# A perceiver block on one core: column term as a single fp32r product, first batch's norm earlier, correction's rows during the attention

## The chip, the cores and the metric

One NeuronCore of a Trainium2 chip runs the whole program as one launch. The metric is the device time of a launch in microseconds (us), median over the runs. TensorE (PE) multiplies, VectorE (DVE) and ScalarE (ACT) do elementwise work and move results out of PSUM, GpSimd (POOL) fills masks, and SyncE (SP) issues nearly all transfers from memory. Each engine works through its own list in order and waits on semaphores.

## The reference, cut to what matters

Two batches of 128 rows by 2048 columns go through three residual steps.

```python
x = x + fake_quant(layernorm(x)) @ fake_quant(ctx)         # ctx: 2 x 2048 x 2048, 33.5 MB of fp32
h = layernorm(x); q = h @ Wq; k, v = split(h @ Wkv)         # 32 heads of 64, one shared k and v
x = x + softmax(q k^T/8 + alibi, causal) v @ Wo
x = x + layernorm(x) @ (scales * (nibbles(qweight) - (nibbles(qzeros) + 1))) + bias
```

`fake_quant` rounds to the integers 0 to 255 and subtracts a zero point z. The kernel works on values shifted by 128, so the true product is that of the shifted integers plus a row term plus a **column term**: (128 - z1) times the column sums of the shifted context. The last step's zero points and bias are added by a small product with the groups' row sums, the **correction**.

## The kernel before, in words

All work is written out by hand as one list per engine.

**First step, contexts.** SP loads 32 context tiles of 128x2048 fp32 (1 MB each) into a ring of eight slots, 16 for each batch. For each, ACT quantises to bytes (`round_ctx`, L411), DVE converts the bytes to bf16 into one of two buffers (`convert_ctx`, L679), and PE runs four 512-column products into the batch's banks (L956) and four 32-row products with ones that gather the column sums in one bank (L963). `convert_ctx(i)` waits for PE to have finished tile i-2; PE's tile i waits for `convert_ctx(i)`.

After a batch's last tile, `colsums(b)` (L685) copies the column sums out, and `zero_point(b)` (L970) multiplies them by a selector `sel` that holds 128 - z1 in one row for each chunk, four fp32 products, adding the column term to the batch's four banks. DVE then adds each chunk to the residual and takes its statistics (`first_residual`, L690 and L597), and normalises (L611).

**Hand over.** `transposes(n)` (L988) turns a normalised batch: 16 transposes in four groups, each group into a bank. ACT copies a group out as its upper fp32r part (`upper`, L424), DVE subtracts for the lower part (`remainder`, L618, which counts `lo_out`). Groups 0 and 3 share a bank for both batches, so the last four transposes wait for the remainder of group 0. For batch 0 they stand between context tiles of batch 1 (before `ctx_tile(1, 8)`); ACT's `upper(0, g)` stand after `round_ctx(25)` and `round_ctx(26)`. For batch 1 they stand between q products.

**Second step.** Weights come as 1 MB granules; ACT makes the upper part (`upper_w`, L433), DVE the lower (`remainder_w`, L627). The first four q granules are multiplied piece by piece: `q_by_upper(w, b)` (L1008, eight products), `q_by_lower(w, b)` (L1015, four). `keys_values` (L1041 to L1048) then forms k and v of both batches. From there a chain runs: DVE copies them out (L760, L761), ACT issues two transfers that double k (L521), waits for them, fills `k_pair` (L526), and only then copies batch 1's q rows out of PSUM (`q_rows(1)`, L443), for which PE's second half of granule 4 waits.

**Output weights and correction.** After the attention POOL zeroes the tiles of the correction (L395, L396, in `work`, where the probabilities were), SP loads zero points and scales (L320, L321) behind the eleventh output granule, DVE unpacks and multiplies them (L884 to L888), SP adds the bias rows (L327), ACT rounds (L565) and DVE splits (L898). PE uses the result at L1171. SP's list is in order, so each of its waits holds what stands behind it.

The last step runs 16 granules of dequantised weights (L1138), made by DVE and ACT, against both batches.

Lines the argument touches in the lists:

```python
for w in range(3):          # PE, L1195
    q_by_upper(w, 0)
transposes(1)
...
q_by_upper(3, 1)            # PE, L1206
keys_values()
q_by_lower(3, 0)
q_by_lower(3, 1)
value_rows()
```

Of the kernel before, what the change touches and what calls it, by code (L numbers as in the profile page):

```python
# [16 lines left out]
B = 2  # L17
# [49 lines left out]
def perceiver(nc, x, ctx_in, s1, z1, s2, z2, wq, wkv, wo, qweight, qzeros, scales, bias, out):  # L67
# [6 lines left out]
    with ExitStack() as ec:  # L74
# [9 lines left out]
        with nc.sbuf_tensor("nib_pad", [P, D], F32), nc.sbuf_tensor("nib_a", [P, D], F32) as nib_a, \  # L84
                nc.sbuf_tensor("raw_fifth", [P, D], F32) as raw_fifth, \
                nc.sbuf_tensor("corr_r", [P, D], F32R) as corr_r:
            pass

# [26 lines left out]
        with nc.sbuf_tensor("sel", [P, NCH, P], F32) as sel:  # L115
            pass
# [31 lines left out]
        part_lo = sb("part_lo", [P, 2], F32)  # L148
        one_row = sb("one_row", [P, 1], F32)
# [4 lines left out]
        colsum_at = work[:, 0, 2 * CH:3 * CH]  # L154
        prob_slots = [work[:, 1, 0:D // 2], work[:, 1, D // 2:D], work[:, 0, D // 2:D]]
        corr = work[:, 0]
        corr_z = work[:, 1]
# [45 lines left out]
        sel_zero = sem("sel_zero")  # L203
# [59 lines left out]
        def tr_bank(n, g):  # L263
            if n == 0:
                return g % 3
            return 1 + g % 3 if n == 1 else 4 * (n % B) + g
# [16 lines left out]
        @block.sync  # L283
        def _(sp):
            sp.dma_start(resid[:, 0, :], x[0]).then_inc(x_loaded[0], 16)
            for i in range(CTX_TILES):
                if i == 6:
                    sp.dma_start(resid[:, 1, :], x[1]).then_inc(x_loaded[1], 16)
                if i >= CTX_RING:
                    sp.wait_ge(ctx_q, i - CTX_RING + 1)  # L290
                sp.dma_start(ctx_slots[i % CTX_RING], ctx_tiles[i]).then_inc(ctx_loaded[i % CTX_RING], 16)

            def load_granule(rows, base, w):
                slot_free(sp, w)
                n, kq = divmod(w - base, 4)
                sp.dma_start(raw_slots[slot_of(w)].rearrange("p (t n) -> p t n", t=4),
                             rows[:, 4 * kq:4 * kq + 4, n * CH:(n + 1) * CH]).then_inc(w_loaded[slot_of(w)], 16)

            for w in range(W_Q, W_O):
                if w < RING:  # L300
                    sp.wait_ge(ctx_q, CTX_TILES - CTX_RING + w + 1)
                if w == RING:
                    sp.wait_ge(a16_set, 2)
                    sp.dma_start(kv_raw[:].rearrange("p (t n) -> p t n", t=KT), wkv_rows).then_inc(wkv_loaded, 16)
                load_granule(wq_rows, W_Q, w)
                if w in (9, 13):
                    h = (w - 9) // 4
                    for i in range(GROUPS // HALVES):
                        g = h * (GROUPS // HALVES) + i
                        sp.dma_start(scale[i * PER_GROUP:(i + 1) * PER_GROUP, h, :],  # L310
                                     scales[g:g + 1, :].to_broadcast([PER_GROUP, D])).then_inc(scales_loaded[h], 16)
            for w in range(W_O, W_O + 11):
                load_granule(wo_rows, W_O, w)


            attention_over(sp)
            sp.wait_ge(corr_zero, 1)
            for blk in range(3):
                r = slice(CBLK * blk, CBLK * blk + GROUPS)
                sp.dma_start(zraw[r, :], qzeros).then_inc(corr_loaded, 16)  # L320
                sp.dma_start(corr[r, :], scales).then_inc(corr_loaded, 16)  # L321
            for w in range(W_O + 11, W_O + 14):
                load_granule(wo_rows, W_O, w)
            sp.dma_start(packed[:, 0, :], qweight[0:P, :]).then_inc(packed_loaded[0], 16)
            sp.wait_ge(corr_set, 1)
            for blk in range(2):
                sp.dma_start(corr[CBLK * blk + GROUPS:CBLK * blk + GROUPS + 1, :],  # L327
                             bias.unsqueeze(0)).then_inc(bias_loaded, 16)
            load_granule(wo_rows, W_O, W_O + 14)
            load_granule(wo_rows, W_O, W_O + 15)  # L330
            sp.dma_start(packed[:, 1, :], qweight[P:2 * P, :]).then_inc(packed_loaded[1], 16)

            for b in range(B):
                for n in range(NCH):
                    c = slice(n * CH, (n + 1) * CH)
                    sp.wait_ge(final_set, NCH * b + n + 1)
                    sp.dma_start(out[b, :, c], resid[:, b, c]).then_inc(stored, 16)
            sp.wait_ge(stored, 16 * B * NCH)

        @block.gpsimd  # L340
        def _(pool):
            steps = [0]

            def link(ins):
# [12 lines left out]
                                    pattern=[[-1, P]], channel_multiplier=1).then_inc(idents_set, 1)  # L357

# [35 lines left out]
            attention_over(pool)  # L394
# [4 lines left out]
        def _(act):  # L399
# [162 lines left out]
            for w in range(W_O + 6, W_O + 14):  # L562
                upper_w(w)
            act.wait_ge(bias_loaded, 16 * 2)
            nc.scalar.activation(corr_r[:], corr, ACT.Copy).then_inc(corr_hi, 1)  # L565
            upper_w(W_O + 14)
            upper_w(W_O + 15)
# [15 lines left out]
        def _(dve):  # L583
# [53 lines left out]
            def selector():  # L637
                dve.wait_ge(prm_set, 1)
                nc.vector.memset(sel[:], 0.0).then_inc(sel_zero, 1)
                dve.wait_ge(sel_zero, 1)  # L640
                for n in range(NCH):
                    r = slice(P // NCH * n, P // NCH * n + 1)
                    ins = nc.vector.tensor_scalar(sel[r, n, :], sel[r, n, :], dif[r, 1:2], None, ALU.add)
                ins.then_inc(sel_set, 1)
# [36 lines left out]
            def colsums(b):  # L681
# [3 lines left out]
                nc.vector.tensor_copy(colsum_at, bank[:, COLSUM_BANK[b], :]).then_inc(colsum_out, 1)  # L685
# [41 lines left out]
            convert_ctx(KT + 3)  # L727
            convert_ctx(KT + 4)
            reciprocal_sd(2)
            normalise(0).then_inc(norm_set, 1)  # L730
            for i in range(5, 8):
                convert_ctx(KT + i)
            for g in range(4):
                remainder(0, g)
                if g < 3:
                    convert_ctx(KT + 8 + g)
            for i in range(11, 14):
                convert_ctx(KT + i)
# [137 lines left out]
            for i in range(7, 11):  # L876
                remainder_w(W_O + i)
# [8 lines left out]
            link(ins)  # L886
            link(nc.vector.tensor_scalar(corr_z[rows, :], zi, -1.0, 7.0, ALU.mult, ALU.add))
            nc.vector.tensor_tensor(corr[rows, :], corr[rows, :], corr_z[rows, :], ALU.mult).then_inc(corr_set, 1)  # L888
            second_residual(1, 0)
# [8 lines left out]
            nc.vector.scalar_tensor_tensor(out=corr_r[:], in0=corr_r[:].bitcast(F32), scalar=part_lo[:, 0:1],  # L898
# [42 lines left out]
        def _(pe):  # L941
# [25 lines left out]
            def zero_point(b):  # L967
                pe.wait_ge(colsum_out, b + 1)
                for n in range(NCH):
                    mm(bank[:, 4 * b + n, :], sel[:, n, :], colsum_at, start=False,  # L970
                       stop=True).then_inc(ctx_done, 1)

            def transposes(n):
                b = n % B
                pe.wait_ge(norm_set, n + 1)
                for t in range(KT):
# [7 lines left out]
                    if n < B and t == 12:  # L984
                        pe.wait_ge(lo_out, 4 * n + 1)
# [201 lines left out]
            for k in range(KT):  # L1187
                if k == KT // 2:
                    transposes(0)
                ctx_tile(1, k)  # L1190
            zero_point(1)

            for w in range(3):  # L1195
# [10 lines left out]
            q_by_upper(3, 1)  # L1206
            keys_values()
            q_by_lower(3, 0)
# [101 lines left out]
```

## Time and profile before

| what | value |
|---|---|
| median of 3 runs (lowest, highest) | 424.68 us (423.73, 426.18) |
| profiled execution: its own time, its span | 425.28 us, 423.4 us |
| PE busy, weight loads busy | 374.8 us (89%), 275.9 us |
| DVE, ACT, POOL busy | 318.5 us, 223.6 us, 9.2 us |
| HBM read, over the span | 74.91 MB, 182 GB/s |
| chain that ended last: PE, DVE, ACT, DMA | 74%, 16%, 4%, 2% |

The span is the profiled execution from its first to its last record; the 1.9 us beside it belong to the launch. Times inside the span are counted from its start. PE's busy time is what the profile models for pipelined matmuls, so it is read together with the idle time ahead of a group, which names what ended the wait. PEclk is the clock granted to TensorE as a share of 2.4 GHz. A record of DVE that doesn't wait starts some 0.08 us before the end of the one ahead, and one that does starts 0.03 to 0.05 us behind what it waits for.

### The profile page before, as it was taken

To read this page: it belongs to the slowest core of one execution; us is meant where nothing else is said; L and a number is where in the kernel's file an instruction comes from. 1 tells how busy PE (TensorE), PEld (TensorE's weight loads), DVE (VectorE), ACT (ScalarE), POOL (GpSimd) and SP (SyncE) were. 2 spreads that over 40 slices of the span, in tenths; PEclk is the share of its full clock that TensorE was granted. 3 is DMA by queue.
4 is the path that set the end of the run, shared out by engine and by line. 5 is a ranking of instruction groups with operands and counts; after the bars stand their busy time and mean duration, and the time that the engine had idled before them with its cause. 6 is when DMAs were issued, how large, how long until landed. Compare 5 with 4: busy or idle time off the path is not lost.

```text
span 423.4 us, 4567 instructions
## 1 busy us (share of the span) xinstructions
PE 374.8 (89%) x1772; PEld 275.9 (65%) x1772; DVE 318.5 (75%) x354; ACT 223.6 (53%) x268; POOL 9.2 (2%) x43
## 2 busy tenths in 40 slices
PE   0167595878898999999999999999999999999996
PEld 0112131325786877877877867888888788888884
DVE  2598989768963394594595786679999899999922
ACT  1898888795334495297377465336605234444000
POOL 6000000000000000000000002000000000000000
PEclk9998999999999999999999999999999999999999
DMA  8999999995083294393436520987400000000033
GB/s 325 426 423 421 418 421 423 420 392 201 4 293 113 99 231 167 123 249 125 167 132 206 190 100 2 318 231 294 195 0 2 0 2 0 0 2 0 2 99 99
DMA packets 24273, 77.43 MB, mean 183 GB/s; under 512 B 1626, under 2 KB 1802, under 8 KB 19210
## 3 DMA queue, kind: packets, MB, share of 16 engines
q1 hardware_dynamic: 24084, 77.01, 50.4%
q8 instruction: 14, 0.23, 0.2%
q10 hardware_dynamic: 168, 0.13, 0.1%
q14 instruction: 7, 0.06, 0.0%
HBM read 74.91 MB, written 2.10 MB: 182 GB/s over the span
## 4 chain that ended last, share of the span: by engine, by line
PE 74%; DVE 16%; ACT 4%; issue 3%; DMA 2%; ACTq 0%; DVEq 0%
PE bank L1138 20%; PE bank L995 12%; PE bank L997 11%; PE bank L996 11%; DVE q L679 5%; PE bank L956 4%; PE bank L1076 3%; DVE stats L597 2%; PE bank L1008 2%; PE bank L1100 2%; ACT q L411 2%; PE bank L1015 2%; PE bank L1088 1%; DMA prm_row<-in_L_xattn_x_zp 1%; DVE resid L690 1%
## 5 line engine op out<-in xcount | busy, mean ns | idle before, releaser
L627 DVE TENSOR_TENSOR w_lo<-raw,w_hi 128x2048 fp32r<-128x2048 f32 x29 | 65.9, 2285 | 12.2 <-ACT w_hi L433 12.2
L433 ACT ACTIVATE w_hi<-raw 128x2048 fp32r<-128x2048 f32 x29 | 55.2, 1912 | 27.8 <-DMA raw<-in_L_attn_Wo 15.6
L1138 PE MATMUL bank<-w_hi,hd 128*128 128x512 f32 x208 | 52.6, 390 | 0.0
L956 PE MATMUL bank<-q,at 128*128 128x512 bf16 x128 | 36.8, 414 | 16.6 <-DVE q L679 16.3
L1138 PEld LDWEIGHTS bank<-w_hi,hd 128*128 128x128 f32 x208 | 39.0, 188 | 8.1
L679 DVE TENSOR_SCALAR q<-q 128x2048 bf16<-128x2048 uint8 x32 | 38.4, 1218 | 6.4 <-PE bank L963 3.6
L995 PE MATMUL bank<-w_hi,xt 128*128 128x512 f32 x96 | 40.1, 417 | 1.6 <-ACT work L443 1.6
L995 PE MATMUL bank<-w_hi,hd 128*128 128x512 f32 x104 | 41.3, 398 | 0.0
L997 PE MATMUL bank<-w_hi,hd 128*128 128x512 f32 x104 | 40.5, 390 | 0.0
L996 PE MATMUL bank<-w_lo,hd 128*128 128x512 f32 x104 | 40.5, 389 | 0.0
L462 ACT ACTIVATE work<-work,neg_mx 128x128 f32<-128x128 f32 x64 | 24.8, 390 | 26.3 <-DVE neg_mx L791 26.1
L997 PE MATMUL bank<-w_hi,xt 128*128 128x512 f32 x96 | 37.6, 391 | 0.0
L996 PE MATMUL bank<-w_lo,xt 128*128 128x512 f32 x96 | 37.4, 390 | 0.0
L411 ACT ACTIVATE q<-raw,prm,inv 128x2048 uint8<-128x2048 f32 x16 | 33.3, 2090 | 2.5 <-DMA raw<-in_ctx 2.4
L411 ACT ACTIVATE q<-ctx_more,prm,inv 128x2048 uint8<-128x2048 f32 x16 | 32.5, 2086 | 1.2 <-DMA ctx_more<-in_ctx 1.2
L956 PEld LDWEIGHTS bank<-q,at 128*128 128x128 bf16 x128 | 10.6, 102 | 34.6 <-DVE q L679 20.5
L783 DVE SCALAR_TENSOR_TENSOR work<-kq,bank 128x128 f32<-128x128 f32 x64 | 13.3, 282 | 22.9 <-PE bank L1076 22.9
L559 ACT ACTIVATE work<-work 128x4096 bf16<-128x4096 uint16 x5 | 18.1, 3615 | 21.9 <-DVE work L858 21.9
L1138 PE MATMUL bank<-w_lo,hd 128*128 128x512 f32 x104 | 28.8, 389 | 0.0
L995 PEld LDWEIGHTS bank<-w_hi,xt 128*128 128x128 f32 x96 | 18.0, 188 | 7.5 <-issue 2.4
L995 PEld LDWEIGHTS bank<-w_hi,hd 128*128 128x128 f32 x104 | 19.5, 188 | 4.7 <-issue 0.8
L997 PEld LDWEIGHTS bank<-w_hi,hd 128*128 128x128 f32 x104 | 19.5, 188 | 4.1
(148 smaller groups left out, 625.0 us busy)
## 6 DMA issues: line engine op xcount, KB each, us to landing
raw<-in_ctx SPq DMA_DIRECT2D x16, 1024.0 KB, 16.8
ctx_more<-in_ctx SPq DMA_DIRECT2D x16, 1024.0 KB, 17.2
raw<-in_L_attn_Wq SPq DMA_DIRECT2D x16, 1024.0 KB, 5.8
raw<-in_L_attn_Wo SPq DMA_DIRECT2D x13, 1024.0 KB, 5.2
raw_fifth<-in_L_attn_Wo SPq DMA_DIRECT2D x3, 1024.0 KB, 7.3
resid<-in_x SPq DMA_DIRECT2D x2, 1024.0 KB, 11.7
scale<-in_L_ffn_scales SPq DMA_DIRECT2D x16, 128.0 KB, 6.7
packed<-in_L_ffn_qweight SPq DMA_DIRECT2D x2, 1024.0 KB, 7.4
```

Source lines behind the costliest of these rows:

```text
L411: nc.scalar.activation(q8[:, i % Q8], ctx_slots[i % CTX_RING], ACT.Identity, bias=prm[:, 3:4], scale=inv[:, 2:3]).then_inc(ctx_q, 1)
L433: nc.scalar.activation(hi_slots[s], raw_slots[s], ACT.Copy).then_inc(w_hi_set, 1)
L462: ins = nc.scalar.activation(prob[:, c], prob[:, c], ACT.Exp, scale=-1.0, bias=neg_mx[:, u % 2, h:h + 1], accum_out=den[:, u % 2, h:h + 1])
L559: nc.scalar.activation(values.bitcast(BF16), values.bitcast(U16), ACT.Copy, bias=-8.0).then_inc(d8_set, 1)
L627: nc.vector.tensor_tensor(lo_slots[s], raw_slots[s], hi_slots[s].bitcast(F32), ALU.subtract).then_inc(w_lo_set, 1)
L679: nc.vector.tensor_scalar(q16[:, i % 2], q8[:, i % Q8], -QSHIFT, None, ALU.add).then_inc(ctx_c, 1)
L783: ins = nc.vector.scalar_tensor_tensor(out=prob[:, c], in0=kq[:], scalar=-sl[2 * PAIRS * g + r], in1=bank[:, SCORE_BANK + r // PAIRS, r % ...
L956: mm(bank[:, 4 * b + n, :], at[:, k, b * P:(b + 1) * P], q16[:, i % 2, n * CH:(n + 1) * CH], start=start, stop=False)
L995: mm(bank[:, out_bank, :], x_hi, hi[:, c], start=first, stop=False)
L996: mm(bank[:, out_bank, :], x_hi, lo[:, c], start=False, stop=False)
L997: return mm(bank[:, out_bank, :], x_lo, hi[:, c], start=False, stop=last)
L1138: return mm(bank[:, 4 * b + n, :], left[:, j, b * P:(b + 1) * P], right[slot_of(W_F + j)][:, n * CH:(n + 1) * CH], start=part == 0 and j = ...
```

## The change: what it does

- `sel` becomes fp32r and is filled in all its rows by another recipe: DVE multiplies ones by a column `sel_col`, which holds the upper part of 128 - z1 in the first row of a block of 32 and its lower part 16 rows further; POOL lays out that pattern at the start. `colsums` is now two linked operations: a copy as fp32r, and one that leaves in the block's rows the column sum less a sixteenth of the row's number (0 to 15) times its upper part. The column term is one fp32r product a chunk in place of an fp32 one.
- PE runs `q_by_upper(0, 0)` ahead of `zero_point(1)`.
- Batch 0's normalisation stands two conversions earlier in DVE's list, its remainders one earlier, and its transposes stand before `ctx_tile(1, 5)`. ACT's list is unchanged there.
- Batch 1's four groups of transposes go to banks 1, 2, 3 and 5, so none waits for another's remainder.
- `q_by_lower(3, 0)` stands ahead of `keys_values`.
- The correction's rows move to memory that is free after the last q product. POOL zeroes them then, SP loads them behind output granule 4, and the bias ahead of granule 12. DVE's three steps stand between the remainders of granules 7 to 10, and ACT's rounding writes `work` ahead of granule 13.

```diff
-        with nc.sbuf_tensor("sel", [P, NCH, P], F32) as sel:
+        with nc.sbuf_tensor("sel", [P, NCH, P], F32R) as sel, nc.sbuf_tensor("colsum_hi", [P, CH], F32R) as colsum_hi, \
+                nc.sbuf_tensor("colsum", [P, CH], F32R) as colsum:
             pass
...
-            return 1 + g % 3 if n == 1 else 4 * (n % B) + g
+            return (1, 2, 3, 5)[g] if n == 1 else 4 * (n % B) + g
...
-            for w in range(W_O, W_O + 11):
+            for w in range(W_O, W_O + 12):
                 load_granule(wo_rows, W_O, w)
-            attention_over(sp)
-            sp.wait_ge(corr_zero, 1)
-            for blk in range(3):
-                r = slice(CBLK * blk, CBLK * blk + GROUPS)
-                sp.dma_start(zraw[r, :], qzeros).then_inc(corr_loaded, 16)
-                sp.dma_start(corr[r, :], scales).then_inc(corr_loaded, 16)
-            for w in range(W_O + 11, W_O + 14):
-                load_granule(wo_rows, W_O, w)
-            sp.dma_start(packed[:, 0, :], qweight[0:P, :]).then_inc(packed_loaded[0], 16)
+                if w == W_O + RING:
+                    sp.wait_ge(corr_zero, 1)
+                    for blk in range(3):
+                        r = slice(CBLK * blk, CBLK * blk + GROUPS)
+                        sp.dma_start(zraw[r, :], qzeros).then_inc(corr_loaded, 16)
+                        sp.dma_start(corr[r, :], scales).then_inc(corr_loaded, 16)
             sp.wait_ge(corr_set, 1)
             for blk in range(2):
                 sp.dma_start(corr[CBLK * blk + GROUPS:CBLK * blk + GROUPS + 1, :],
                              bias.unsqueeze(0)).then_inc(bias_loaded, 16)
+            for w in range(W_O + 12, W_O + 14):
+                load_granule(wo_rows, W_O, w)
+            attention_over(sp)
+            sp.dma_start(packed[:, 0, :], qweight[0:P, :]).then_inc(packed_loaded[0], 16)
...
+            nc.gpsimd.iota(row_no[:], pattern=[[0, 1]], base=0, channel_multiplier=1).then_inc(sel_rows, 1)
+            link(nc.gpsimd.memset(sel_at[:], 0.0))
+            for part in range(2):
+                for half in range(2):
+                    link(nc.gpsimd.affine_select(out=sel_at[:, part], in_=sel_at[:, part], compare_op=ALU.not_equal,
+                                                 fill=1.0, base=-(part + 16 * half), pattern=[[-P // NCH, NCH]],
+                                                 channel_multiplier=1))
+            nc.gpsimd.memset(sel_col[:], 0.0).then_inc(sel_rows, 1)
...
-            attention_over(pool)
+            pool.wait_ge(k_dup, 2 * 16)
+            pool.wait_ge(w_used, USED.index(W_O - 1) + 1)
             link(nc.gpsimd.memset(zraw.bitcast(F32), 0.0))
             nc.gpsimd.memset(corr, 0.0).then_inc(corr_zero, 1)
...
-            for w in range(W_O + 6, W_O + 14):
+            for w in range(W_O + 6, W_O + 13):
                 upper_w(w)
             act.wait_ge(bias_loaded, 16 * 2)
-            nc.scalar.activation(corr_r[:], corr, ACT.Copy).then_inc(corr_hi, 1)
-            upper_w(W_O + 14)
-            upper_w(W_O + 15)
+            attention_over(act)
+            nc.scalar.activation(corr_up, corr, ACT.Copy).then_inc(corr_hi, 1)
+            for w in range(W_O + 13, W_O + 16):
+                upper_w(w)
...
             def selector():
-                dve.wait_ge(prm_set, 1)
-                nc.vector.memset(sel[:], 0.0).then_inc(sel_zero, 1)
-                dve.wait_ge(sel_zero, 1)
+                dve.wait_ge(sel_rows, 2)
+                link(nc.vector.tensor_scalar(row_no[:], row_no[:], 16, None, ALU.bitwise_and))
+                nc.vector.tensor_scalar(lower_row[:], row_no[:], -1.0 / 16, None, ALU.mult)
+                link(nc.vector.tensor_copy(dif_hi[:], dif[:, 1:2]))
+                link(nc.vector.tensor_tensor(dif_lo[:], dif[:, 1:2], dif_hi[:].bitcast(F32), ALU.subtract))
+                link(nc.vector.tensor_scalar(sel_col[:], sel_at[:, 1], dif_lo[:], None, ALU.mult))
+                link(nc.vector.scalar_tensor_tensor(out=sel_col[:], in0=sel_at[:, 0], scalar=dif_hi[:].bitcast(F32),
+                                                    in1=sel_col[:], op0=ALU.mult, op1=ALU.add))
                 for n in range(NCH):
-                    r = slice(P // NCH * n, P // NCH * n + 1)
-                    ins = nc.vector.tensor_scalar(sel[r, n, :], sel[r, n, :], dif[r, 1:2], None, ALU.add)
+                    ins = nc.vector.tensor_scalar(sel[:, n, :], ones16[:], sel_col[:, n:n + 1], None, ALU.mult)
                 ins.then_inc(sel_set, 1)
...
-                nc.vector.tensor_copy(colsum_at, bank[:, COLSUM_BANK[b], :]).then_inc(colsum_out, 1)
+                link(nc.vector.tensor_copy(colsum_hi[:], bank[:, COLSUM_BANK[b], :]))
+                nc.vector.scalar_tensor_tensor(out=colsum[:], in0=colsum_hi[:].bitcast(F32), scalar=lower_row[:],
+                                               in1=bank[:, COLSUM_BANK[b], :], op0=ALU.mult,
+                                               op1=ALU.add).then_inc(colsum_out, 1)
...
             convert_ctx(KT + 2)
-            convert_ctx(KT + 3)
-            convert_ctx(KT + 4)
             reciprocal_sd(2)
             normalise(0).then_inc(norm_set, 1)
-            for i in range(5, 8):
+            for i in range(3, 7):
                 convert_ctx(KT + i)
             for g in range(4):
                 remainder(0, g)
                 if g < 3:
-                    convert_ctx(KT + 8 + g)
-            for i in range(11, 14):
+                    convert_ctx(KT + 7 + g)
+            for i in range(10, 14):
                 convert_ctx(KT + i)
...
-            for i in range(7, 11):
-                remainder_w(W_O + i)
+            remainder_w(W_O + 7)
...
+            remainder_w(W_O + 8)
             link(nc.vector.tensor_scalar(corr_z[rows, :], zi, -1.0, 7.0, ALU.mult, ALU.add))
+            remainder_w(W_O + 9)
             nc.vector.tensor_tensor(corr[rows, :], corr[rows, :], corr_z[rows, :], ALU.mult).then_inc(corr_set, 1)
+            remainder_w(W_O + 10)
...
-                    if n < B and t == 12:
-                        pe.wait_ge(lo_out, 4 * n + 1)
+                    if n == 0 and t == 12:
+                        pe.wait_ge(lo_out, 1)
...
-                if k == KT // 2:
+                if k == 5:
                     transposes(0)
                 ctx_tile(1, k)
+            q_by_upper(0, 0)
             zero_point(1)
-            for w in range(3):
+            for w in range(1, 3):
                 q_by_upper(w, 0)
             transposes(1)
...
             q_by_upper(3, 1)
+            q_by_lower(3, 0)
             keys_values()
-            q_by_lower(3, 0)
             q_by_lower(3, 1)
```

## Rows read from the trace of the kernel before

**Rows 1.** The page's first line: span of the profiled execution.
```profile
span 423.4 us, 4567 instructions
```

**Rows 2.** Windows: busy us of PE, PEld, DVE, ACT, POOL; clock; DMA share; GB/s.
```profile
67.00:76.00 9.00, 6.75 (x42) 2.07 (x41) 8.06 (x12) 8.40 (x5) 0.00 (x0) 1.00 1.01 422
76.00:95.60 19.60, 15.36 (x95) 5.77 (x92) 12.77 (x13) 16.72 (x13) 0.00 (x0) 1.00 1.02 403
```

**Rows 3.** Timeline of ACT: start, duration, operation, idle before and its releaser.
```profile
73.97 2.10 ACT L411 ACTIVATE q<-raw,prm,inv 128x2048 uint8<-128x2048 f32 x1 [0.40 <-DMA raw<-in_ctx]
78.94 1.08 ACT L424 ACTIVATE xt<-bank 128x512 fp32r<-128x512 f32 x2 [2.88 <-PE bank L988]
...
86.82 6.07 ACT L411 ACTIVATE q<-ctx_more,prm,inv 128x2048 uint8<-128x2048 f32 x3
```

**Rows 4.** PE's longest wait from 244 to 345 us: in all, times, longest.
```profile
PE bank L1132 <- DVE hd L618: 1.0, 1, 1.0
```

**Rows 5.** Timeline of all engines behind batch 1's last context tile.
```profile
95.63 0.69 DVE L685 COPY work<-bank 128x512 f32<-128x512 f32 x1 [1.48 <-PE bank L963]
...
96.37 3.70 PE L970 MATMUL bank<-work,sel 128*128 128x512 f32 x8 [0.80 <-DVE work L685]
...
97.53 0.75 DVE L690 SCALAR_TENSOR_TENSOR resid<-bank,ss,resid 128x512 f32<-128x512 f32 x1 [1.22 <-PE bank L970]
...
99.51 6.04 PE L1008 MATMUL bank<-w_hi,xt 128*128 128x512 f32 x24
```

**Rows 6.** The same timeline, from keys and values to batch 1's q rows.
```profile
129.60 0.42 DVE L760 COPY kv_t<-bank 128x256 f32<-128x256 f32 x1 [1.88 <-PE bank L1045]
...
130.50 0.60 ACT L443 ACTIVATE work<-bank 128x512 f32<-128x512 f32 x1 [5.11 <-PE bank L1015]
130.51 1.16 ACTq L521 DMA_DIRECT2D k_t<-kv_t  x2
...
136.57 0.47 PE L995 MATMUL bank<-w_hi,xt 128*128 128x512 f32 x1 [1.55 <-ACT work L443]
```

**Rows 7.** Timeline of DVE from batch 0's column term to its normalisation.
```profile
60.06 0.75 DVE L690 SCALAR_TENSOR_TENSOR resid<-bank,ss,resid 128x512 f32<-128x512 f32 x1
...
69.74 1.23 DVE L679 TENSOR_SCALAR q<-q 128x2048 bf16<-128x2048 uint8 x1 [0.42 <-PE bank L963]
...
71.58 1.35 DVE L611 TENSOR_SCALAR work<-resid,mv,rstd 128x2048 f32<-128x2048 f32 x1
```

**Rows 8.** Timeline of PE in batch 1's context tiles.
```profile
66.14 0.40 PE L963 MATMUL bank<-q,ones 128*32 128x512 bf16 x4 [2.68 <-DVE resid L690]
...
74.12 1.04 PE L956 MATMUL bank<-q,at 128*128 128x512 bf16 x4 [1.73 <-DVE q L679]
...
80.32 0.72 PE L988 MATMUL bank<-ident,work 128*128 128x128 f32 x4 [0.51 <-DVE xt L618]
```

**Rows 9.** Timeline of DVE and PE at batch 1's transposes.
```profile
105.73 2.29 DVE L627 TENSOR_TENSOR w_lo<-raw,w_hi 128x2048 fp32r<-128x2048 f32 x1
...
105.86 1.62 PE L988 MATMUL bank<-ident,work 128*128 128x128 f32 x12 [0.31 <-DVE work L611]
...
108.67 0.71 PE L988 MATMUL bank<-ident,work 128*128 128x128 f32 x4 [1.18 <-DVE xt L618]
```

**Rows 10.** Timeline of PE: two context tiles behind idle time.
```profile
38.23 1.89 PE L956 MATMUL bank<-q,at 128*128 128x512 bf16 x4 [2.39 <-DVE q L679]
...
51.84 1.89 PE L956 MATMUL bank<-q,at 128*128 128x512 bf16 x4 [2.10 <-DVE q L679]
```

**Rows 11.** Windows of PE alone: its busy us, granted clock, DMA share, GB/s.
```profile
38.00:39.00 1.00, 0.77 (x2) 0.50 1.00 418
...
40.00:41.00 1.00, 1.00 (x7) 0.50 1.06 442
```

**Rows 12.** Timeline of DVE and ACT among the output weights.
```profile
266.50 2.27 DVE L627 TENSOR_TENSOR w_lo<-raw,w_hi 128x2048 fp32r<-128x2048 f32 x1
...
285.44 1.92 ACT L433 ACTIVATE w_hi<-raw 128x2048 fp32r<-128x2048 f32 x1 [0.93 <-DMA raw<-in_L_attn_Wo]
...
285.72 2.29 DVE L888 TENSOR_TENSOR work<-work 96x2048 f32<-96x2048 f32 x1
```

More of the change, by code:

```diff
@@ L87, in perceiver @@
             pass
+        with nc.sbuf_tensor("corr_pad", [P, 3, D], F32), nc.sbuf_tensor("corr_rows", [P, D], F32) as corr_rows:
+            pass
         xt = sb("xt", [P, 2, KT, B * P], F32R)
@@ L148, in perceiver @@
         part_lo = sb("part_lo", [P, 2], F32)
+        row_no = sb("row_no", [P, 1], I32)
+        lower_row = sb("lower_row", [P, 1], F32)
+        sel_at = sb("sel_at", [P, 2, NCH], F32)
+        sel_col = sb("sel_col", [P, NCH], F32)
+        dif_hi = sb("dif_hi", [P, 1], F32R)
+        dif_lo = sb("dif_lo", [P, 1], F32)
         one_row = sb("one_row", [P, 1], F32)
         q_rows_at = [work[:, 0, 0:CH], work[:, 0, CH:2 * CH]]
-        colsum_at = work[:, 0, 2 * CH:3 * CH]
         prob_slots = [work[:, 1, 0:D // 2], work[:, 1, D // 2:D], work[:, 0, D // 2:D]]
-        corr = work[:, 0]
-        corr_z = work[:, 1]
+        corr = corr_rows[:]
+        corr_z = nib_a[:]
+        corr_up = work[:, 0].bitcast(F32R)
         nib_slots = [nib_a[:], work[:, 0], work[:, 1]]
@@ L202, in perceiver @@
         ctx_mm = sem("ctx_mm")
-        sel_zero = sem("sel_zero")
+        sel_rows = sem("sel_rows")
         sel_set = sem("sel_set")
@@ L897, in _ @@
             dve.wait_ge(corr_hi, 1)
-            nc.vector.scalar_tensor_tensor(out=corr_r[:], in0=corr_r[:].bitcast(F32), scalar=part_lo[:, 0:1],
+            nc.vector.scalar_tensor_tensor(out=corr_r[:], in0=corr_up.bitcast(F32), scalar=part_lo[:, 0:1],
                                            in1=corr, op0=ALU.mult, op1=ALU.add).then_inc(corr_split, 1)
@@ L969, in zero_point @@
                 for n in range(NCH):
-                    mm(bank[:, 4 * b + n, :], sel[:, n, :], colsum_at, start=False,
+                    mm(bank[:, 4 * b + n, :], sel[:, n, :], colsum[:], start=False,
                        stop=True).then_inc(ctx_done, 1)
```

## The prediction

> **What bounds the kernel.** The span [rows 1] is 1.9 us below the profiled execution's own 425.28 us, and that execution is 0.6 us above the median of 424.68. I read the windows first. To 76 us the transfers run at full share, 422 GB/s [rows 2], so a context tile of 1.049 MB lands each 2.49 us. ACT's timeline shows two things [rows 3]: tile 25 still waits for its transfer (0.40 us), but then ACT stands idle for 2.88 us until batch 0's transposes arrive, and the last three tiles are quantised back to back to 92.9. So the context stage ends on ACT, though its transfers would allow an earlier end. From 136.57 on, PE is the bound: 0.8 us of waiting at 247, 1.0 us near 333 [rows 4], little else. The change can therefore gain only ahead of 136.57, and what stands there comes through whole: behind the last tile DVE's chain of residual, statistics and norm [rows 5], then the transposes, then keys and values and the doubling of k, behind which PE waits 1.55 us [rows 6].
>
> **Selector.** Ten small DVE operations replace five, near 25 us. None can take more than the 0.42 us of a 128x256 copy [rows 6], so 0 to 2.1 us more; I take 0.5, since most are on one column. It delays DVE ahead of 76 us, where the step after next finds 0.5 us of cover. POOL's additions precede 5 us and nobody waits for them.
>
> **Batch 0's column term.** The copy of 0.69 us [rows 5] gets a second operation. Not in the trace; the nearest row is the residual's, also 512 columns with one PSUM input, 0.75 [rows 7]. With the link: 1.52 in place of 0.70. The first chunk took 1.14 us in fp32 (96.37 to 97.51 [rows 5]); an fp32r product takes 0.47 [rows 6]. DVE's first residual moves from 60.06 to about 60.6 [rows 7], as `convert_ctx(16)` stands between.
>
> **Batch 0's norm and transposes.** Two conversions and a wait ahead of the norm drop out, 1.15 + 1.15 + 0.42 = 2.7 us [rows 7], so it starts at 71.58 + 0.6 - 2.7 = 69.5 and ends at 70.8. Four conversions follow, paced by PE's tiles (1.4 us each); tile 20 ends at 74.8, and there the transposes start; the last four began at 80.32 before [rows 8]. Group 0 is there at 75.5, ACT is free at 76.07: its 2.88 us of waiting goes. ACT then needs 4 x 0.49 for the groups and 1.99 a tile: it reaches tile 31 at 88.4, which lands at 73.96 + 6 x 2.49 = 88.9, and is done at 91.0, against 92.9. That is 1.9 us, if nothing else is late.
>
> DVE and PE are. `convert_ctx(23)` now waits for tile 21, which stands **behind** the transposes; before, the conversion there needed a tile long done. Remainder 0 ends at 77.3, the last four transposes at 78.0 (0.72 [rows 8]), tile 21 at 79.4. From there DVE runs four conversions and three remainders, 4 x 1.15 + 3 x 0.6 = 6.4, to 85.8; four more go at PE's pace of 1.4, to 91.5; conversion 31 and tile 31 take 2.7 more: 94.2, against 95.6. **Gain 1.4**, between 0 and 1.9.
>
> **Batch 1's column term.** `q_by_upper(0, 0)` takes 1.81 us (24 products in 5.4 [rows 5]) and hides the two DVE operations (1.52). The first chunk is there 1.84 + 0.45 = 2.3 us behind the tile, against 1.96 (97.53 less 95.57). PE itself saves much: four fp32 products took 3.14 us (96.37 to 99.51), fp32r ones take 0.9. But the norm is DVE's chain of 8.3 us from the first residual (97.53) to 105.81 [rows 5, 9], which doesn't change. It ends at 94.2 + 2.3 + 8.3 = 104.8: gain 1.05, and the 2.2 us saved on PE become idle time: PE has nothing from 100.9 to 104.8, 3.9 us where it had 0.31 [rows 9].
>
> **Fourth bank.** The last four transposes waited 1.18 us for a remainder behind DVE's 2.29 us of `remainder_w(0)` [rows 9]. That wait goes; PE reaches `q_by_upper(0, 1)` about 1.3 us earlier in its own count, just as the fourth remainder is done. Gain 1.3.
>
> **Keys and values.** PE resumes 7.0 us behind the end of `keys_values` (129.56 to 136.57 [rows 6]): two copies, two transfers, `k_pair`, `q_rows(1)`. Before, `q_rows(0)` and the transfer's issue came within 0.01 us of each other (130.50, 130.51), so earlier q rows free nothing. With four products of 0.226 ahead of it, `keys_values` ends 0.9 us later: **loss 0.9**, and PE's idle time there grows from 1.55 to 2.5.
>
> **The clock.** With the clock at its upper level all this is 1.05 + 1.3 - 0.9 = 1.5 us faster. But PE lay idle 2.39 and 2.10 us before the tiles at 38.23 and 51.84, whose four products took 1.89 us in place of 1.04 [rows 10], at a granted clock of 0.50, that is 1.2 GHz, for about 3 us [rows 11]; idle times of 2.68 and 1.73 us cost nothing [rows 8]. In the new kernel 3.9 us ahead of batch 1's transposes is longer than any of these: I take the fall to 1.2 GHz as given. Three us at half pace lose up to 1.7, some of it behind DVE's remainders: I take 1.3 (0.6 to 1.7). At 2.5 us, behind k, it is open; there PE is the bound and a fall costs 1.2 to 1.7 in full. A third idle time, some 5 us, comes in tile 16 (PE done sooner, waiting for the residual [rows 8]); its slow tiles are covered, since the norm stands between on DVE.
>
> The Trainium skill ("TensorE: Matmul & The Clock Gate", Why this matters for your kernels) advises against idle gaps of PE between bursts in mid kernel because the clock falls back. It speaks against this change, which makes three such gaps; the trace agrees at 38.23 and 51.84.
>
> **Correction.** Nothing: PE never waited for it. DVE's 10.3 us of corr work and three remainders now start behind granule 7's (266.50 + 2.27) and set `corr_set` near 279.7 against 288.0 [rows 12]. SP holds granule 12 back by at most 2.7 us for it; its upper part at 285.44 becomes 288, and DVE takes its lower part only after 290. If that cover is gone, up to 2.7 us are at risk. POOL's fill runs in the attention near 224, where DVE has idle time.
>
> **Sum.** 1.4 - 0.3 + 1.3 - 0.9 - 1.3 = +0.2 us of gain: 425.1 against the profiled execution, 424.5 against the median. I forecast **424.6**.
>
> **The rivals.** 0.5% is 2.1 us, about what a measurement of this kernel can tell.
> - **One fall of the clock** (the forecast), chance 0.38: 424.6, own range 423.9 to 425.4.
> - **A second fall**, in the 2.5 us behind k, chance 0.27: 1.5 us worse, 426.1. For it: falls behind 2.39 and 2.10 us. Against: none behind 2.68.
> - **The clock holds**, chance 0.15: 1.5 us faster than before, 423.2. For it only that 2.68 us did no harm.
> - **Everything hides** (faster): DVE keeps up to the transfers (1.9 in place of 1.4), the clock holds, and the earlier `q_rows(0)` lets ACT issue k's transfers sooner, so that nothing is lost at k. 1.9 - 0.3 + 1.3 = 2.9: 421.8. Chance 0.1.
> - **Slower**: PE's clock at k. It falls in the 2.5 us and stays low for all of the next 3.4 us of q products (loss 1.7), after the first fall cost its full amount and one remainder more (2.3): 1.5 - 2.3 - 1.7 = -2.5, 427.2. It decides once both losses sum over 3.6 us. Chance 0.1; for it the row at 38.23, against it that DVE's remainders hide part of the first.
>
> **How the numbers follow.** The range reaches from everything hiding to nearly the last rival: 421.9 to 426.9. Faster by over 0.5%: 0.1 and a little of the held clock, 0.12. Slower: 0.1 and the upper edge of the second fall, 0.12. The rest, 0.76, is no change.
>
> **What would show it.** ACT without a wait for L988 before tile 26; the last context product ending near 94.2 and waiting for DVE's conversions from tile 23 on; two DVE operations of 0.7 us each at the column sums; PE idle 3 to 4 us before batch 1's transposes, with clock 0.50 behind it; no wait inside them; PE idle near 2.5 us ahead of granule 4's second half. I would be wrong if the last tile ended where it did before, if that idle time left the clock at 1.0, or if PE waited at granules 12 to 15.

## The result, and the profile after

The changed kernel takes **430.64 us** in the median of 4 runs (429.51 to 431.27), the kernel before 424.26 in 4 runs beside it; ratio 1.0121, interval 1.0082 to 1.0161. It is slower by 1.2%, outside the forecast's range of 421.9 to 426.9; the two medians alone are 6.4 us (1.5%) apart, and that too lies within the interval. The profiled execution took 430.05 us; its span is 4.9 us longer than before [rows 1]. From the page of the changed kernel, its first line, PE's busy time and the granted clock by slices:

```profile
span 428.3 us, 4567 instructions
PE 376.5 (88%) x1759; PEld 277.7 (65%) x1764; DVE 320.5 (75%) x361; ACT 224.3 (52%) x268; POOL 10.2 (2%) x50
...
PEclk9998997699899899999999999999999999999999
```

PE's busy time hardly changed (376.5 us, before 374.8); below 9 the clock row shows where it ran slowly. What PE waited for in the changed kernel (us in all, times, longest):

```profile
PE bank L993 <- DVE resid L720: 4.8, 1, 4.8
PE bank L1018 <- DVE work L634: 4.1, 1, 4.1
PE bank L1025 <- ACT work L465: 3.8, 1, 3.8
PE bank L1018 <- DVE xt L641: 3.4, 1, 3.4
```

These are four places, in order of time the residuals in tile 16 (4.8, before 2.68 [rows 8]), batch 0's transposes (3.4, before 0.51), batch 1's transposes (4.1, before 0.31 and 1.18 [rows 9]) and k (3.8, before 1.55 [rows 6]). Behind 146 us the waits are those of before, 0.8 and 1.0 us [rows 4]: everything was lost ahead of it.

**Contexts.** PE's timeline of the changed kernel, where L986 and L993 are a tile's products and L1018 the transposes:

```profile
64.30 0.62 PE L993 MATMUL bank<-q,ones 128*32 128x512 bf16 x4 [4.82 <-DVE resid L720]
64.85 1.89 PE L986 MATMUL bank<-q,at 128*128 128x512 bf16 x4
...
67.22 1.89 PE L986 MATMUL bank<-q,at 128*128 128x512 bf16 x4
...
72.36 1.62 PE L1018 MATMUL bank<-ident,work 128*128 128x128 f32 x12
77.39 1.12 PE L1018 MATMUL bank<-ident,work 128*128 128x128 f32 x4 [3.41 <-DVE xt L641]
...
80.70 1.89 PE L986 MATMUL bank<-q,at 128*128 128x512 bf16 x4
```

Here the clock falls twice, and each time there are tiles of 1.89 us. The transposes start at 72.36, well ahead of ACT, whose first copy of them comes at 76.03 behind tile 25; PE waits for the remainder made from it, then runs tiles 21 and 22 slowly. DVE's next conversion waits 3.56 us for tile 21, as the second timeline shows:

```profile
76.64 0.69 DVE L641 TENSOR_TENSOR xt<-bank,xt 128x512 fp32r<-128x512 f32 x1 [2.86 <-ACT xt L446]
80.89 1.23 DVE L706 TENSOR_SCALAR q<-q 128x2048 bf16<-128x2048 uint8 x1 [3.56 <-PE bank L993]
...
96.28 0.69 DVE L712 CAST colsum_hi<-bank 128x512 fp32r<-128x512 f32 x1 [1.48 <-PE bank L993]
```

ACT is done with the contexts near 91.1, 1.8 us sooner than before, but the last tile ends at 96.23, 0.6 later.

**Batch 1's transposes.** All 16 in one piece, but behind 4.06 us of idle time and mostly at the lower clock (0.50 in the windows from 108 to 110): 3.34 us, where 16 transposes at full pace take 2.1 (the run with filling products below shows them at this same place).

```profile
98.11 1.07 PE L1000 MATMUL bank<-colsum,sel 128*128 128x512 f32 x4
...
106.86 3.34 PE L1018 MATMUL bank<-ident,work 128*128 128x128 f32 x16 [4.06 <-DVE work L634]
```

**k.** Timeline of all engines of the changed kernel, and the windows behind it (PE's busy us, clock, DMA share, GB/s):

```profile
131.69 0.42 DVE L788 COPY kv_t<-bank 128x256 f32<-128x256 f32 x1 [2.70 <-PE bank L1075]
...
132.58 0.37 SPq L305 DMA_DIRECT2D raw<-in_L_attn_Wq  x1
132.60 1.16 ACTq L543 DMA_DIRECT2D k_t<-kv_t  x2
...
138.56 0.85 ACT L548 ACTIVATE k_pair<-k_t 64x256 f32<-64x256 f32 x2 [2.83 <-DMA k_t<-kv_t]
...
140.18 0.47 PE L1025 MATMUL bank<-w_hi,xt 128*128 128x512 f32 x1 [3.83 <-ACT work L465]
```
```profile
140.00:141.00 1.00, 0.82 (x4) 1.00 0.00 0
141.00:142.00 1.00, 1.00 (x5) 0.76 0.09 16
142.00:143.00 1.00, 1.00 (x3) 0.50 0.00 0
143.00:144.00 1.00, 1.00 (x4) 0.50 0.00 0
144.00:145.00 1.00, 1.00 (x7) 0.53 0.00 0
```

SP's load of granule 7 goes into the slot that `q_by_lower(3, 1)` frees, the call that now stands right behind `keys_values`. Before, SP issued the load 0.9 us behind k's first transfer; now it goes 0.02 us ahead of it, and `k_pair` starts 5.96 us behind the issue in place of 4.44 [rows 6]. PE lies idle for 3.83 us and the clock falls behind it.

**The account.** Profiled execution against profiled execution: last context tile +0.6; norm of batch 1 (105.81 to 106.82) +1.0; end of `keys_values` (129.56 to 131.65) +2.1; PE's return behind k (136.57 to 140.18) +3.6; the second half of granule 4, mostly at the lower clock, 4.3 us (140.18 to 144.50 on the chain) in place of 3.0 (136.57 to 139.58), +4.9; the four transposes behind it, 0.7 us in place of 0.4, +5.2. Some 0.3 of that is made up later; the spans differ by 4.9.

### The profile page after: what moved, and what is told of

It is laid out like the page before. It is cut to its first block, busy times and chain, and to the rows that moved or that the text cites. A ratio compares the mean times of both kernels' runs of the same rounds, so it can differ in the third digit from the quotient of the medians.

```text
span 428.3 us, 4567 instructions
## 1 busy us (share of the span) xinstructions
PE 376.5 (88%) x1759; PEld 277.7 (65%) x1764; DVE 320.5 (75%) x361; ACT 224.3 (52%) x268; POOL 10.2 (2%) x50
## 4 chain that ended last, share of the span: by engine, by line
PE 71%; DMA 15%; DVE 8%; ACT 3%; issue 2%; ACTq 0%; DVEq 0%
PE bank L1168 20%; DMA raw<-in_ctx 12%; PE bank L1025 12%; PE bank L1027 11%; PE bank L1026 11%; PE bank L1106 3%; PE bank L1038 3%; PE bank L1130 2%; PE bank L986 2%; PE bank L1018 2%; PE bank L1045 1%; ACT q L433 1%; PE bank L1118 1%; DVE q L706 1%; DMA k_t<-kv_t 1%
## 5 line engine op out<-in xcount | busy, mean ns | idle before, releaser
L986 PE MATMUL bank<-q,at 128*128 128x512 bf16 x123 | 39.5, 448 | 10.4 <-DVE q L706 9.3
L1025 PE MATMUL bank<-w_hi,xt 128*128 128x512 f32 x96 | 40.5, 422 | 3.8 <-ACT work L465 3.8
L1027 PE MATMUL bank<-w_hi,xt 128*128 128x512 f32 x96 | 38.2, 398 | 0.0
L986 PEld LDWEIGHTS bank<-q,at 128*128 128x128 bf16 x128 | 11.2, 108 | 30.1 <-DVE q L706 13.0
```

Of the source, the lines that this page charges most:

```text
L986: mm(bank[:, 4 * b + n, :], at[:, k, b * P:(b + 1) * P], q16[:, i % 2, n * CH:(n + 1) * CH], start=start, stop=False)
L1025: mm(bank[:, out_bank, :], x_hi, hi[:, c], start=first, stop=False)
L1027: return mm(bank[:, out_bank, :], x_lo, hi[:, c], start=False, stop=last)
```

## The experiments

Theory K after the result: most of the loss sits at k, as 0.9 us of PE's order, 1.5 us because granule 7's megabyte is under way in the same 16 DMA engines, and 1.5 us of clock. Rival N: it is made ahead of k. All runs stand beside runs of the kernel before on the same chip, whose medians were 424.4 to 425.0 us; its single runs there reach from 422.1 to 427.6. The changed kernel wasn't run again beside them: differences to its 430.64 are taken to the runs of the section above.

### 1. The order at k, undone in the changed kernel and done alone in the one before

```diff
-            q_by_lower(3, 0)
             keys_values()
+            q_by_lower(3, 0)
             q_by_lower(3, 1)
```

> The changed kernel with q_by_lower(3, 0) behind keys_values again. Theory K (most of the loss sits at k): keys_values ends 0.9 us sooner, granule 7's load is issued after k's transfers' first part rather than with them (k doubled in 3.9 us in place of 5.4), the wait ahead of granule 4's second half falls from 3.8 to about 1.5 us and the clock stays at 1.0 behind it (1.5 us): together 3.9 us, 430.6 becomes about 426.7. Rival N (the loss is made ahead of k, by the slow clock at the contexts and at batch 1's transposes, and the order at k only moves it about): at most 0.9 us, about 429.7.

Measured: **424.75** us (10 runs, 423.45 to 425.12), before 424.68; ratio 0.9992 (0.997 to 1.0015). All of the loss is gone, 5.9 us, two more than expected. In its trace k's transfers no longer share their start with the granule; `k_pair` starts 3.05 us behind the issue, right behind an upper part that ACT was busy with, and PE doesn't wait at k at all. What the rest of the change costs ahead of k is still there: `keys_values` ends at 131.21, 1.65 us later than in the profile of before, which then waited 1.55 us for k. The lines at k:

```profile
132.16 1.17 ACTq L543 DMA_DIRECT2D k_t<-kv_t  x2
133.38 1.92 ACT L455 ACTIVATE w_hi<-raw 128x2048 fp32r<-128x2048 f32 x1 [0.63 <-issue]
135.21 0.84 ACT L548 ACTIVATE k_pair<-k_t 64x256 f32<-64x256 f32 x2
```

Then the same move, added to the kernel before and nothing else.

> The kernel before with that one call moved ahead of keys_values, nothing else. Theory K: 0.9 + 1.5 (transfer) + 1.5 (clock), 424.3 becomes about 428.2, and the trace shows k's transfers landing 5.4 us after the first issue, PE idle near 4 us and clock 0.50 behind it. Rival N: 0.9 at most, 425.2.

Measured: **428.64** us, before 424.68; ratio 1.0092 (1.0061 to 1.0122): 4.0 us, as theory K had it. The lines show each term: granule and k issued together, 6.04 us to `k_pair`, 3.92 us of idle PE, and behind it a clock of 0.50 in the windows from 141 to 143.

```profile
131.39 0.37 SPq L296 DMA_DIRECT2D raw<-in_L_attn_Wq  x1
131.40 1.16 ACTq L521 DMA_DIRECT2D k_t<-kv_t  x2
...
137.44 0.85 ACT L526 ACTIVATE k_pair<-k_t 64x256 f32<-64x256 f32 x2 [2.92 <-DMA k_t<-kv_t]
...
139.06 0.47 PE L995 MATMUL bank<-w_hi,xt 128*128 128x512 f32 x1 [3.92 <-ACT work L443]
```

Rival N falls as the main cause: one moved call of four products makes two thirds of the loss by itself, and putting it back removes all of it.

### 2. The clock's share

```diff
+            def filler(count, at_bank):
+                for _ in range(count):
+                    mm(bank[:, at_bank, :], ones16[:], q16[:, 1, 0:CH], start=True, stop=True)
...
+            filler(14, 1)
             transposes(1)
...
+                if n == 1:
+                    filler(12, 3)
                 q_granule(w, 1)
```

> The changed kernel with products that nobody reads where PE waits: 14 of 512 columns ahead of batch 1's transposes and 12 ahead of granule 4's second half, all inside the idle time. Theory K, clock part: both falls go, the transposes run in 2.1 instead of 3.3 us and the q products behind k at full pace; 1.0 to 1.5 at each place, 430.6 becomes about 427.9; the waits themselves stay. If the clock were no cause, 430.6 or later.

Measured: **425.99** us, ratio to before 1.0029 (0.9999 to 1.006): 4.6 us less than the changed kernel, where 2.7 were expected. Both falls are gone. The transposes take 2.07 us and k still lands after 5.97:

```profile
106.02 2.07 PE L1018 MATMUL bank<-ident,work 128*128 128x128 f32 x16 [1.03 <-DVE work L634]
```
```profile
136.18 0.85 ACT L548 ACTIVATE k_pair<-k_t 64x256 f32<-64x256 f32 x2 [2.85 <-DMA k_t<-kv_t]
...
137.80 0.47 PE L1025 MATMUL bank<-w_hi,xt 128*128 128x512 f32 x1 [1.26 <-ACT work L465]
```

The spans differ by 3.8 us: 0.9 at the contexts (last tile at 95.4 in place of 96.2), which the filler doesn't touch and which varies with where the falls there begin; 1.5 from the norm to the end of `keys_values` (23.30 us in place of 24.83), 1.3 of it the transposes; and 1.6 from PE's return behind k to the end of the transposes there (3.44 us in place of 5.03), less 0.2 made up later. The two falls alone account for 3.1 us of it; the waits stayed, and are now filled. So products that nobody reads, placed in idle time, are worth time here.

### 3. The transfer's share

```diff
             def load_granule(rows, base, w):
                 slot_free(sp, w)
+                if w == 7:
+                    sp.wait_ge(k_dup, 2 * 16)
```

> The changed kernel with SP holding q granule 7's load until k's two transfers have landed. Theory K, transfer part: k lands 3.9 us after its issue in place of 5.4, PE resumes 1.5 us sooner; its idle time is then 2.5 us, so the clock may hold too: 430.6 becomes 429.1, or 427.6 if it holds. If the 5.4 us had another cause than the granule in the same 16 engines: 430.6.

Measured: **425.61** us, ratio 1.0023 (0.9995 to 1.0051). With the granule held back, `k_pair` follows the issue by 3.04 us, again right behind ACT's other work, and k landed before 135.53, where SP lets the granule go; the wait of PE is 0.88 us and the clock behind it holds.

```profile
132.87 1.17 ACTq L545 DMA_DIRECT2D k_t<-kv_t  x2
...
135.53 0.37 SPq L307 DMA_DIRECT2D raw<-in_L_attn_Wq  x1
135.91 0.83 ACT L550 ACTIVATE k_pair<-k_t 64x256 f32<-64x256 f32 x2
```

The view of `k_t` gives the time from issue to landing of the two transfers (lowest, median, highest), here in this order for this run, the changed kernel, the run of the column term below (granule 7 issued 0.9 us behind k) and the kernel before (the same 0.9):

```profile
DMA to landing us min/median/max: 1.9/2.0/2.0
DMA to landing us min/median/max: 5.3/5.3/5.4
DMA to landing us min/median/max: 1.9/2.0/2.1
DMA to landing us min/median/max: 1.9/2.9/3.9
```

So the granule issued with k costs each transfer 3.3 us, and PE 3.0 us of waiting (3.83 less 0.88), not the 1.5 that I had taken from the profile of before, whose second transfer was itself late. The transfer's term also brings the clock's with it: 3 us of idle time less, and no fall.

### 4. The other parts, each alone in the kernel before

The column term (selector, two operations, fp32r products, `q_by_upper(0, 0)` ahead):

> The kernel before with the fp32r column term alone (selector, two operations for the column sums, q_by_upper(0, 0) ahead of it). Theory C (PE's shorter work only lengthens its waits, and the clock falls in them): batch 1's norm ends 0.3 us later, PE is idle near 4 us ahead of batch 1's transposes where it had 0.3, clock 0.50 behind it, 1.0 to 1.5 us lost; another fall behind the wait for the residuals in tile 16. 424.7 becomes 425.7 to 426.5. Rival P (2.2 us less of PE work is worth something): 422.5 to 424.

Measured: **425.88** us, before 424.99; ratio 1.0043 (1.0014 to 1.0073). PE is idle for 4.06 us ahead of the transposes and they take nearly double:

```profile
107.25 3.92 PE L1012 MATMUL bank<-ident,work 128*128 128x128 f32 x16 [4.06 <-DVE work L628]
```

The same with the 14 filling products ahead of the transposes:

> The fp32r column term alone, as in the fifth run, with 14 products of 512 columns that nobody reads ahead of batch 1's transposes. If the fall of the clock there is what made that run 1.2 us slower than before (theory C), the transposes take 2.1 us again, the 425.9 becomes 424.4 and the clock's fall behind tile 16 stays, at no cost. If the two operations for the column sums or the selector are the cause, it stays near 425.9.

Measured: **424.8** us, before 424.43; ratio 1.0019 (0.9986 to 1.0052). The transposes are back to their times of before, with the old wait of 1.18 us among them, so the clock has a share in the loss: `keys_values` ends 0.9 us sooner than without the filling products (130.75 in place of 131.68). The times alone don't settle it: the medians are 1.1 us apart, 0.5 when each is taken against its own runs of before, and the two intervals overlap.

```profile
107.22 1.62 PE L1012 MATMUL bank<-ident,work 128*128 128x128 f32 x12 [1.02 <-DVE work L628]
110.02 0.72 PE L1012 MATMUL bank<-ident,work 128*128 128x128 f32 x4 [1.18 <-DVE xt L635]
```

Batch 0's norm and transposes (`k == 5`, with DVE's list as changed):

> The kernel before with batch 0's norm two conversions earlier and its transposes before tile 21 alone. PE then stands idle inside the transposes until ACT, bound by tile 25's transfer, has copied group 0: 2.5 to 3.4 us, as in the changed kernel. Theory C: with the fp32 column term in place the clock still falls there, two or three tiles run slowly, and the last tile ends within 0.8 us of where it did (95.6): 424.0 to 425.2. Rival (what the prediction said): last tile at 94.2, 1.4 us faster, 423.3.

Measured: **424.51** us, before 424.99; ratio 0.9977 (0.9943 to 1.0011), not told apart from no change. PE waits 3.3 us inside the transposes, the clock falls in the windows from 77 to 81, and the last tile ends at 95.5, where it did.

The fourth bank:

```diff
-            return 1 + g % 3 if n == 1 else 4 * (n % B) + g
+            return (1, 2, 3, 5)[g] if n == 1 else 4 * (n % B) + g
...
-                    if n < B and t == 12:
-                        pe.wait_ge(lo_out, 4 * n + 1)
+                    if n == 0 and t == 12:
+                        pe.wait_ge(lo_out, 1)
```

> The kernel before with banks 1, 2, 3 and 5 for batch 1's transposes alone. The wait of 1.18 us before the last four goes and nothing else changes, clock at 1.0: keys_values ends 1.2 us sooner, 424.7 becomes 423.5. Rival: DVE's remainders are the bound there and it stays within 0.3 us.

Measured: **422.92** us, before 424.99; ratio 0.9958 (0.9927 to 0.999). All 16 transposes run in one piece, and in this execution k landed early enough that PE didn't wait for it:

```profile
106.07 2.08 PE L988 MATMUL bank<-ident,work 128*128 128x128 f32 x16 [0.31 <-DVE work L611]
```

The correction's rows:

> The kernel before with the correction's rows moved alone. PE waited for nothing there and no new wait of PE appears behind 140 us: 424.7, within 0.3. Rival: SP's list, held by the filled tiles and by corr_set, delays weights: PE waits at output granules 12 to 15, or DVE slows beside POOL's fill in the attention, 1 to 3 us slower.

Measured: **424.78** us, before 424.99; ratio 1.0013 (0.9978 to 1.0048). Nothing, and PE's waits behind 140 us are the same two.

### 5. What beats both kernels

ACT copied batch 1's q rows only after its wait for k, though they don't need k:

```diff
             upper_w(6)
+            q_rows(1)
             act.wait_ge(k_dup, 2 * 16)
...
-            q_rows(1)
```

In the kernel before, with the fourth bank:

> Before with the fourth bank, and with ACT's copy of batch 1's q rows ahead of its wait for k's transfers. PE then no longer depends on k's landing ahead of granule 4's second half: its wait there (1.55 us in the profile of before, none in some others) is gone in every run. 422.9 of the bank alone becomes about 422.2. Rival: the copy only delays k_pair and the scores; no gain.

Measured: **421.66** us (420.82 to 422.74), before 424.43; ratio 0.9936 (0.9914 to 0.9958). PE doesn't wait at k.

With batch 0's transposes one tile earlier as well, and its norm two conversions earlier:

```diff
             convert_ctx(KT + 2)
-            convert_ctx(KT + 3)
-            convert_ctx(KT + 4)
...
-            for i in range(5, 8):
+            for i in range(3, 8):
...
-                if k == KT // 2:
+                if k == 7:
```

> The same, with batch 0's norm two conversions earlier and its transposes one tile earlier than before (ahead of tile 23, not 21), so that no conversion waits for a tile behind the transposes. ACT should meet them less than 1.5 us late in place of 2.9, and the last tile should end 0.5 to 1.4 us sooner: 421.3. Rival: the clock falls in the tiles ahead, or ACT's wait for the transposes is as long as before; no gain on the run beside it.

Measured: **420.7** us (6 runs, 420.37 to 420.96), before 424.43; ratio 0.9925 (0.9891 to 0.9959): faster than both kernels, 3.7 us below the one before. ACT meets the transposes 0.96 us late where it was 2.88, and the last tile ends at 93.6, so here the 1.9 us that the transfers allow are all had:

```profile
76.97 1.08 ACT L424 ACTIVATE xt<-bank 128x512 fp32r<-128x512 f32 x2 [0.96 <-PE bank L986]
```
```profile
93.66 0.69 DVE L685 COPY work<-bank 128x512 f32<-128x512 f32 x1 [1.48 <-PE bank L961]
```

Its step over the run beside it, 1.0 us in the medians, lies within the two intervals. The q rows' copy in the changed kernel, all else as changed:

> The changed kernel with ACT's copy of batch 1's q rows ahead of its wait for k's transfers; the order of keys_values, the load of granule 7 and all else as changed. Theory K says the order at k costs only through that one wait: k may land 6 us after its issue as before, but PE goes on at once, so its wait of 3.8 us, the clock's fall behind it and the 0.9 us of keys_values' delay all vanish: 430.6 becomes 424.5, within 0.7 of the run with q_by_lower(3, 0) put back (424.75). Rival: the late k is waited for again at the first scores, some 6 us further on, and 1 us or more remains.

Measured: **424.75** us, before 424.61; ratio 1.0008 (0.9976 to 1.004), 5.9 us below the changed kernel with the order at k untouched. `k_pair` still starts 5.9 us behind the issue, but the copy no longer stands behind it:

```profile
131.41 1.15 ACTq L543 DMA_DIRECT2D k_t<-kv_t  x2
...
134.43 0.58 ACT L465 ACTIVATE work<-bank 128x512 f32<-128x512 f32 x1
...
137.29 0.86 ACT L549 ACTIVATE k_pair<-k_t 64x256 f32<-64x256 f32 x2 [2.28 <-DMA k_t<-kv_t]
```

The late k is not waited for at the first scores; PE has one new wait of 0.8 us, for ACT's copy of the transposed q. Of the 5.7 us between the two spans 1.2 are had ahead of k (DVE copies it at 130.49, in the changed kernel at 131.69), by contexts that ended sooner in this execution; the other 4.5 lie at k and behind it. So the order at k costs nearly all through that one wait on ACT.

## Why the prediction was wrong

**Keys and values, the step that failed.** It said "loss 0.9, and PE's idle time there grows from 1.55 to 2.5", from a chain of 7.0 us taken as fixed. The 0.9 was right: in the kernel before with that one call moved, DVE copies k at 130.49 in place of 129.60. The chain wasn't fixed: its longest link is a transfer, and the moved call also changes when SP may issue the next megabyte. That term, 1.5 us by the two profiles (5.3 in place of 3.9 to landing) and 3.3 against a transfer left alone (2.0), was missing. I had followed what the call's move does on PE and ACT, and not its semaphore: `q_by_lower(3, 1)` frees a slot, and SP waits for it. In the sum for the profiled execution, forecast at 425.1 and measured at 430.05, this term is 1.5 us, the second fall of the clock 1.6, the contexts 2.0 (last tile at 96.2 in place of 94.2) and the step from the norm to the end of `keys_values` 0.2, less 0.3 made up later.

**The second fall of the clock** was a rival with a chance of 0.27 since 2.5 us of idle time was between the cases seen. It came in both profiles with that wait at full length (the changed kernel and the move alone, 3.8 and 3.9 us, costing 1.6 us in the first), and not in the run with 0.9, nor with the filler. "None behind 2.68" left out a row of the same trace: the first context tile, also behind 2.68 us of idle time, took 1.87 us, though the clock row reads 1.00 there. The range's slow end held this fall but not the transfer, so it ended at 426.9.

**Contexts, wrong on the size and, in the profile, the sign.** "Gain 1.4", with the last tile at 94.2; it came at 96.2 in the profile. The step "the norm stands between on DVE" for the slow tiles behind tile 16 held: DVE waited 0.23 us for them. What failed is that the transposes start when PE gets to them and end when ACT has copied group 0: I had them start at 74.8, 1.3 us ahead of their first copy; they started at 72.4, 3.7 ahead of it, and behind the wait of 3.4 us inside them the clock was low on the very tiles that DVE's next conversions need. The last run above, with the changed kernel's lists up to here, shows the forecast's case: its transposes start at 74.2, PE waits 1.60 us inside them, the clock stays at 1.00, and the last tile ends at 94.1.

```profile
77.41 0.71 PE L1018 MATMUL bank<-ident,work 128*128 128x128 f32 x4 [1.60 <-DVE xt L641]
```

So the step that failed here is the clock, which the forecast had at its upper level behind the transposes; the other four profiles with these lists (the changed kernel and the runs with the order undone, with the filling products and with the load held back) end the last tile at 95.4 to 96.4. ACT did end at 91.1 as forecast (91.0). Moved alone this part is worth nothing; moved to tile 23, where a conversion doesn't need a tile behind the transposes, it gave 1.9 at the last tile.

**Batch 1's column term** went by its steps: 0.69 and 0.75 us on DVE, the norm 10.6 us behind the last tile (10.59), PE idle for 4.06 (3.9), the transposes slow. The step from the norm to the end of `keys_values` was forecast at 24.7 us (23.75, less 1.3 for the bank, more 1.3 for the clock and 0.9) and measured 24.83. Alone it costs 0.9 us by the medians.

**Fourth bank**: 1.3 forecast, 2.1 measured alone with a width of 1.3 either way; right in sign, and the one part that earned something. **Selector**: 0.5 forecast, 0.26 measured (1.68 us before, 1.94 after). **Correction**: nothing, as forecast.

The parts alone add up to 0.9 - 0.5 - 2.1 - 0.2 + 4.0 = 2.1 us, against 5.9 to 6.4 measured together. About half of what is missing lies at k: without the move the changed kernel skips the wait there altogether (the run with the order undone), so that in it the move costs 5.9 and not 4.0. The other half isn't placed: the four other parts add up to -1.9 us alone and to 0.1 together in that run, and each of the four is known to about 1.3 us either way. Why k's second transfer landed after 3.9 us in the profile of before and 3.2 in that of batch 0's part alone, but after 2.0 to 2.1 in seven others, with the granule 0.9 us behind in all nine, is not settled; in the profile of before it decides the 1.55 us of waiting, and it may be part of the spread between runs of that kernel.

## What to carry to other kernels

When a call is moved, follow every semaphore that it or its new neighbour raises, and above all those that let a transfer go: a megabyte issued at the same moment as a small transfer that engines wait for costs more than the products moved. An engine that isn't the bound there shouldn't be given less work for its own sake; ask what its idle time does to the clock behind it, and take out the wait instead. A result that doesn't depend on a late arrival should stand ahead of the wait for it in its engine's list: one moved line (`q_rows(1)`) made the order at k harmless.

## What the hardware showed that I had not expected

- k's two transfers of 64 KB each took 2.0 us from issue to landing with nothing beside them, and as long in seven profiles with 1 MB issued 0.9 us behind; in two others the second took 3.2 and 3.9. With the megabyte issued 0.01 to 0.02 us ahead, both took 5.0 to 5.5, in each of four profiles.
- The same idle time brings a fall of the clock or doesn't, and the fall can come late. All 14 profiles have 2.39 us of idle time ahead of tile 7: in three the clock fell at once (tile 7 took 1.7 to 1.9 us), in four it fell one tile later (in the changed kernel tile 7 took 1.04 us and tile 8 1.89), in seven not at all. Behind 1.74 us, ahead of tile 10, three profiles show a slow tile at once.
- Products that nobody reads, in idle time, made a kernel faster: 14 of them by 0.5 to 1.1 us (medians), 26 by 3.1 us at the two places where they stood.
